# Splitting low-rank factors ahead of rescaling, summing x3 with its bias early, building rope tables on VectorE one round ahead, and turning the first queries among the embedding groups

## The reference

```python
x = x + L0_ffn(L0_cond(x, itok))          # weights picked by index, then an int4 matrix
x = x + L1_ffn(L1_cond(x, block_table, cache_seqlens))   # paged attention, then top-1 low-rank
x = x + L2_ffn(L2_cond(x, itok))          # indexed low-rank, then SiLU gate with low-rank terms
x = x + L3_ffn(L3_cond(x, language_ids))  # top-2 experts, then an int8 product

def L1_cond(x):                           # 32 query heads, 8 key/value heads, D = 128
    q, k, v = x @ Wq.T, x @ Wk.T, x @ Wv.T
    q, k = rope(rmsnorm(q, qw), pos), rope(rmsnorm(k, kw), pos)
    # rope: concat(t1 * cos - t2 * sin, t2 * cos + t1 * sin)
    keys, vals = concat(k_cache[block_table], k), concat(v_cache[block_table], v)
    return softmax(mask(q @ keys.T / sqrt(D))) @ vals @ Wo.T

def L3_ffn(t):                            # per-row int8 quantisation
    iscale = max(|t|) / 127
    q = clip(round(t / iscale), -127, 127)
    return (q @ qweight) * iscale * wscale + bias
```

## Time and profile before

| what | value |
|---|---|
| median of 3 runs | 3198.6 us (3192.68 to 3199.76) |
| the profiled execution: its time | 3195.55 us |
| its span, first to last instruction | 3193.8 us |
| PE busy | 3024.6 us, 95% of the span |
| DVE / ACT / POOL busy | 1552.8 / 1284.7 / 1490.8 us |
| mean granted TensorE clock | 0.981 |

### The profile page before, as it was taken

The page is one execution under the profiler, slowest core; times in us unless marked ns, Lnnn a source line. Parts: engine busy times, 40 slices in busy tenths (PEclk is TensorE's granted clock), DMA queues, the critical chain, the costliest instruction groups (busy, mean ns, idle before and its releaser), DMA issues. The chain is left out here.

```text
span 3193.8 us, 55792 instructions
## 1 busy us (share of the span) xinstructions
PE 3024.6 (95%) x15256; PEld 2022.0 (63%) x15264; DVE 1552.8 (49%) x3979; ACT 1284.7 (40%) x3014; POOL 1490.8 (47%) x1275
## 2 busy tenths in 40 slices
PE   3789999999999999999999999999999996999897
PEld 2466666666666666666666666666666674655554
DVE  5544444444444444444444444444444453656665
ACT  1344444444444444444444444444444441222222
POOL 7355555555555555555555555555555540000000
PEclk9899999999999999999999999999999998999998
DMA  8544444444444344545444444434444454211210
GB/s 291 203 115 122 121 121 121 121 119 120 118 118 118 118 118 118 198 119 169 122 119 119 119 119 119 119 119 119 119 119 119 119 150 164 49 40 31 49 30 13
DMA packets 416154, 377.54 MB, mean 118 GB/s; under 512 B 83427, under 2 KB 347763, under 8 KB 414996
## 3 DMA queue, kind: packets, MB, share of 16 engines
q1 hardware_dynamic: 358484, 186.81, 20.7%
q0 software_dynamic: 50480, 174.40, 17.5%
q10 hardware_dynamic: 7056, 14.46, 1.2%
HBM read 341.23 MB, written 25.85 MB: 115 GB/s over the span
## 5 line engine op out<-in xcount | busy, mean ns | idle before, releaser
L533 DVE CUSTOM_DVE_ANT_0 ps_s<-ps_s,mask 128x544 f32<-128x544 f32 x512 | 375.0, 733 | 940.6 <-PE ps_s L360 781.2
L262 POOL DMA_INDIRECT v_sb<-in_v_rows_w,v_row x504 | 489.7, 972 | 473.9 <-PE ps_oT L385 264.2
L319 PE MATMUL ps_t<-wqkv,xT 128*128 128x512 f32 x1488 | 701.6, 594 | 0.0
L383 PEld LDWEIGHTS ps_oT<-pT,v_sb 128*128 128x128 f32 x4096 | 528.4, 192 | 188.9 <-issue 188.2
L433 ACT ACTIVATE ps_s<-ps_s,nmax 128x544 f32<-128x544 f32 x512 | 352.3, 688 | 586.3 <-DVE nmax L533 519.9
L383 PE MATMUL ps_oT<-pT,v_sb 128*128 128x128 f32 x4096 | 543.1, 276 | 11.6 <-issue 11.5
L343 PE MATMUL ps_t<-wo,oT 128*128 128x512 f32 x1024 | 524.7, 596 | 2.5 <-ACT oT L448 0.9
L359 PE MATMUL ps_s<-k_sb,qT 128*128 128x416 f32 x1024 | 448.0, 519 | 11.4 <-issue 5.7
L448 ACT ACTIVATE oT<-ps_oT 128x128 f32<-128x128 f32 x512 | 142.7, 279 | 685.9 <-PE ps_oT L385 656.4
L543 DVE TENSOR_SCALAR p_sb<-ps_s,rinv 128x544 f32<-128x544 f32 x512 | 401.4, 784 | 23.8 <-DVE rinv L540 0.3
L368 PEld LDWEIGHTS ps_pT<-ident_sb,p_sb 128*128 128x128 f32 x2048 | 251.7, 141 | 187.4 <-issue 181.6
(11 more groups left out here) (219 smaller groups left out, 3545.5 us busy)
## 6 DMA issues: line engine op xcount, KB each, us to landing
k_sb<-in_kT SPq DMA_DIRECT2D x2048, 64.0 KB
v_sb<-in_v_rows_w,v_row POOLq DMA_INDIRECT x512
v_new<-v_raw SPq DMA_DIRECT2D x128, 64.0 KB, 1.9
wo<-in_wo_w POOLq DMA_DIRECT2D x2, 4096.0 KB, 15.2
y_scratch<-y_sb SPq DMA_DIRECT2D x32, 256.0 KB
xT<-x1T_scratch POOLq DMA_DIRECT2D x31, 256.0 KB
tab<-rope_scratch POOLq DMA_DIRECT2D x31, 256.0 KB
wqkv<-in_wqkv_w ACTq DMA_DIRECT2D x6, 1024.0 KB, 10.5
```

What stands on the lines that cost most here:

```text
L262: e.indirect_dma_start(out=v_sb[:, b % 2, c, :], out_offset=None, in_=A["v_rows_w"], in_offset=bass.IndirectOffsetOnAxis(ap=v_row[:, b, c: ...
L319: m = e.matmul(ps_t[bank_of(t)][:, :], xT[:, k, :], wqkv[:, k, 512 * t:512 * t + 512], start=k == 0, stop=k == KC - 1)
L383: e.matmul(ps_oT[:, :], v_sb[:, b % 2, c, h * D:(h + 1) * D], pT[:, u % 2, c, :], start=c == 0, stop=False)
L533: e.tensor_tensor_reduce(out=scores(u), in0=scores(u), in1=mask[:, b % 2, :], scale=-SCALE, scalar=3e38, op0=ALU.add, op1=ALU.min, accum_o ...
```

## The change

In the tail `split_low_rank(k + 1, p)` stands before `rescale(k, 1)`; x3 plus bias goes to a new tile `xb` while the next products run; `output(k, p)` is a single add and stands in pass k + 1, between `route` and `third`. SP issues the y loads ahead of the stores.

In the attention VectorE multiplies cosine and sine (`csn`, 64 KB a round, loaded where `tab` of 256 KB was) by the norm weights `w4`, in unit 1 of the round before the one that uses them (`make_tables`). In the embedding GpSimd no longer makes tables: ScalarE squares and scales the cosine, one store takes both, and VectorE makes the first table at g = 2. The angles wait for their own two loads and not for six, the first `spread` stands ahead of the unpacking, `x1` has three buffers, `turn` runs two groups behind, and the page loads and weight sums come earlier. The first round's five query and key tiles are turned by TensorE within the embedding, through two banks, and the waits for the stores of the stage move into the next stage. Clearing `v_new` moves from VectorE to GpSimd. Page numbers lie in four partitions.

```diff
+def make_tables(e, W, cosine, sine):
+    for i, t in enumerate((cosine, sine)):
+        part = lambda v: v[:, :, :].rearrange("p (s b) (h n) -> p s b h n", b=2, h=2)[:, :, i, :, :]
+        e.tensor_tensor(part(W.tab), t.unsqueeze(1).unsqueeze(1).broadcast_to([P, 2, 2, D // 2]), part(W.w4), ALU.mult).then_inc(W.tab_made, 1)
...
-            for t in range(NQT):
-                turn_q(0, t)
             score(0, 0, 0)
...
+            def table(r):
+                e.wait_ge(dma_tab, 16 * r)
+                e.wait_ge(rope_step, STEPS * r)
+                make_tables(e, W, csn[:, 0, :], csn[:, 1, :])
+
             def body(r):
                 for u in range(UNITS):
+                    if u == 1 and not last(r):
+                        table(r + 1)
                     if ahead(r, u, 2) is not None:
                         mask_scores(*ahead(r, u, 2))
...
-    PAGES_AT = {5: (0, 0), 6: (0, 1), 7: (0, 2), 8: (0, 3), 9: (1, 0), 10: (1, 1), 11: (1, 2), 12: (1, 3)}
-    SUMS_AT = {10: ("w2f", "w2"), 12: ("b2f", "b2")}
+    PAGES_AT = {3: (0, 0), 4: (0, 1), 5: (0, 2), 6: (0, 3), 7: (1, 0), 8: (1, 1), 9: (1, 2), 10: (1, 3)}
+    SUMS_AT = {7: ("w2f", "w2"), 8: ("b2f", "b2")}
...
-            e.wait_ge(out_fold, 32)
-            for i in range(2):
-                e.wait_ge(out_x[i], 16 * (GROUPS // 2))
-                e.wait_ge(out_xT[i], 16 * (GROUPS // 2))
...
-            tables(0)
             gather(2)
-            e.wait_ge(out_tab, 16)
-            tables(2)
+            e.wait_ge(trig, 4)
+            e.dma_start(tab_d.rearrange("g p k n -> p k g n"), cs_sn).then_inc(out_tab, 16)
...
+            def turn_q(t):
+                e.wait_ge(W.rope_step, STEPS1 if t < 3 else STEPS)
...
-                if g > 0:
-                    turn(g - 1)
+                if g > 1:
+                    turn(g - 2)
...
+                if g == GROUPS - 1:
+                    for t in range(3):
+                        turn_q(t)
+            turn(GROUPS - 2)
             turn(GROUPS - 1)
+            for t in range(3, NQT):
+                turn_q(t)
...
+            e.activation(cs, cs, ACT.Square).then_inc(trig, 1)
+            e.wait_ge(trig, 3)
+            e.activation(cs, cs, ACT.Copy, scale=-2.0, bias=1.0).then_inc(trig, 1)
...
-            e.wait_ge(dma_t, 16 * 6)
+            e.wait_ge(dma_a, 16 * 2)
...
+            e.wait_ge(bd_zero, 1)
+            spread(0)
             e.wait_ge(dma_q, 16 * 5)
...
-                wait(e, out_x[i], 16 * (g // 2))
-                wait(e, x1_turned, g - 1)
-                e.tensor_tensor(x1[:, i, :], xa[:, g % XB, :], s16[:, i, :], ALU.add).then_inc(x1_ready, 1)
+                wait(e, out_x[g % 3], 16 * (g // 3))
+                wait(e, x1_turned, g - 2)
+                e.tensor_tensor(x1[:, g % 3, :], xa[:, g % XB, :], s16[:, i, :], ALU.add).then_inc(x1_ready, 1)
...
+                for p in both:
+                    e.wait_ge(event["x3_ready"], 2 * k + p + 1)
+                    e.tensor_tensor(xb[p][:, :], x3[p][:, :], bias3[:, :], ALU.add).then_inc(event["x3_biased"], 1)
...
-                e.tensor_tensor(qf[p][:, :], qf[p][:, :], bias3[:, :], ALU.add).then_inc(event["d_biased"], 1)
-                e.wait_ge(event["d_biased"], 2 * k + p + 1)
+                e.wait_ge(event["x3_biased"], 2 * k + p + 1)
                 e.wait_ge(stored[p], 16 * (k + 1))
-                e.tensor_tensor(outb[p][:, :], qf[p][:, :], x3[p][:, :], ALU.add).then_inc(event["out_ready"], 1)
+                e.tensor_tensor(outb[p][:, :], qf[p][:, :], xb[p][:, :], ALU.add).then_inc(event["out_ready"], 1)
...
+                if not (isinstance(k, int) and k == 0):
+                    for p in both:
+                        output(k - 1, p)
                 third(k)
...
-                output(k, 0)
-                rescale(k, 1)
-                output(k, 1)
-                if more:
                     for p in both:
                         split_low_rank(k + 1, p)
+                rescale(k, 1)
```

## The result

The changed kernel takes 3136.16 us (median of 4 runs, 3134.53 to 3139.89) against 3198.47 for the kernel before beside it, ratio 0.9826 [0.9806, 0.9846]. It is faster by 62 us, where 73.4 (76 against the median) was forecast: the time lies in the range, 14 us above the predicted 3122. The profiled run took 3137.39 us, 58.2 less than the profiled run of before.

A forecast was written before the change was run, and what follows sets the result against it. Attention was taken as TensorE's own time, so gains had to come from TensorE's idle time in embedding and tail. Embedding 43.0, tail 30.4 and attention 0 sum to 73.4 us off 3195.55, giving 3122, range 3110 to 3140.

The forecast's parts named there:

- 3.9 less 0.4: Tail's end: pass 7 gains 3.9 us from the earlier gate work; the first last store, later by one add, costs 0.4.
- Both covers: Tail: existing VectorE waits hide the moved output adds (1.38 against 1.36 us) and the xb adds (1.38 in 2.39).
- rival 2: Tail: covers fail, adds costing 1.4 us a pass, or VectorE's gate work limits; gain 21, 3132 us; chance 0.10.
- Rival 3: Attention: GpSimd holds VectorE's table operations, 6.7 us in each of 31 rounds, 207 in all; 3329 us; chance 0.02.
- (b): Embedding, first product to first projection: held add and store wait give back 10.1 us, slow work 1.9; 12.0, from 8 to 14.
- (d): Embedding, last projection to first score: shorter wait 4.5 us, turning 7.5, earlier page issues 5; 17.0, from 11 to 20.
- (a): Embedding, up to the first product: it comes at 29.5 us, 14.0 earlier; 17.5 if ScalarE is no obstacle.
- The other term, 1.9: Embedding, within (b): estimated gain of 1.9 us because part of TensorE's work behind the hold ran slow.
- (c): Embedding: the six projections, 73.72 to 101.93 us, repeat unchanged; gain 0.
- The 5 for the groups: Embedding, within (d): earlier page issues free 5 us of 7.9 idle after the projections, bounds 0 and 7.9.
- The sign named in advance: Embedding: the prediction is wrong if TensorE waits for xa, stores or the fold weights between 30 and 100 us.
- rival 1: Embedding held elsewhere: DMA-bound stretch at 396 GB/s has no slack; gain about 27 us, 3138 us; chance 0.19.

The follow-up runs named there:

- experiments 2 and 3: Kernel before with only the tail's split moved, outputs left: 3171.21 us; kernel before with all tail edits plus eight unused semaphore increments ahead of the tail's loop: 3158.85 us.
- tail_only: Kernel before with all of the change's tail edits and none of the others: 3174.89 us, ratio 0.9953.
- Experiment 6: Changed kernel with ScalarE's Exp and its table load moved ahead of the last turned-query copies (group 15): 3137.42 us, ratio 0.9831.
- The last experiment: Changed kernel with five x buffers, later wqkv loads spread behind mix copies, and ScalarE's table load at group 11: 3119.39 us, ratio 0.9768.
- experiments 5 and 8: Changed kernel with wqkv loads spread behind mix copies: 3130.84 us; the same with five x buffers and ScalarE's table load at group 11: 3119.39 us.

## Why the prediction was right in part

**Tail, 30.4 forecast, 31.3 measured: right, term by term.** Passes 1 to 6 lost 26.1 (26.9 forecast by the length of pass 0), the end 4.6 (3.5 forecast, 3.9 less 0.4), and 0.7 lies ahead of pass 0, where nothing was forecast. Both covers held: passes with the output in front of their x3 add are 0.14 us longer than pass 0, which has none, so rival 2 is out. That both the split and the gate's start matter was argued then and is shown by experiments 2 and 3. It held for the layout that the changed kernel happened to have: in the layout of `tail_only` the same edits gave 17.3, and the prediction did not think of this.

**Attention, 0 forecast: right within the scatter.** Rival 3, the table held by GpSimd, is out: all 62 operations took 0.41 to 0.42 us. That the first profile had 4.5 us more misled me for one round of experiments, since one profile of this stage is worth no more than 6 us either way.

**Embedding, 43.0 forecast, 31.4 measured: the step that failed, (b) and (d).** (a) came as worked out, 30.05 against 29.5, with ScalarE's six issues, which end at 29.35, as the limit that the prediction named.

In (b), 43.50 to 73.72 became 30.05 to 54.37, 5.9 saved of 12.0. The sum gave TensorE the whole hold of VectorE and its wait for a store, 10.1. But TensorE's own row says that it stood 5.63 us for that add; ahead of this it had stood 3.79, until 53.70, for group 4's x, and VectorE's wait and hold began within that time. The 5.63 went and the wait for x grew from 3.79 to 4.83, since the buffer is free only when group 0 is summed: TensorE's idle time fell by 5.7, from 10.5 to 4.8. The other term, 1.9 for slow work behind the hold, gave 0.2 (19.73 to 19.49 us of work), as the work behind the remaining wait was slow again. With a fifth buffer the stretch is 17.1 us long and saves 13.1, which is what shows the wait for x as the cause.

(c) was 28.13 against 28.21. In (d), from the last projection's start to the first score, 43.34 became 31.35: 12.0 saved of 17.0. The 5 for the groups came, 5.1 by the rows of TensorE (28.7 to 23.5, the two turns counted that now stand between the queries'), though only about 1 of it from the waits for x, 5.25 to 4.28; the prediction took the idle time there for the page issues'. What failed is the end: of 12.0 forecast for the wait and the turns (14.66 us before) 6.9 came. A wait of 4.98 was to become a bare meeting of 0.5 and is 4.24. The meeting is 0.45 indeed, but 2.3 us of ScalarE's copies stand ahead of it, and 1.5 of its table load with the operation behind it, an edit of the diff that the sum passed over. Experiment 6 takes that 1.5 off the end. What the copies would give back was not tried.

The last experiment gets 41.1 of the forecast 43.0, but not by the forecast's terms: (b) saves 14.2 there and (d) 13.7. The sign named in advance, TensorE waiting for `xa` between 30 and 100 us, did appear. The mechanism left out was rival 1's, a wait elsewhere, and its 3138 us is nearer to the measured 3136 than the forecast's 3122. Its reason, that the stretch at 396 GB/s has no slack, does not hold: the wait went with as many GB/s, and experiments 5 and 8 ran the stretch from 20 to 50 us at 315 and 319.

In the whole, the stages explain the profiled run: 31.4 and 31.3 less 4.5 are its 58.2. That embedding and tail alone, 62.7, come so close to the medians' 62.3 is partly luck: on two other chips the gain was 58.1 and 63.4.

## What to carry to other kernels

Time for which one engine is held is not time for which the next one waits: before a hold is given back, read the idle time in the rows of the engine that ends the chain, and what else it waits for meanwhile. When a stall goes, ask for each load behind it when it is issued, not only how many bytes there are: a ring of buffers ties the load to the work of so many groups earlier, and work that comes sooner meets it. Work off the path (a table load, an output) is free only where its engine waits for another; look for that idle time in the timeline, not at a place that is early. Before a few microseconds of a long stage are explained, profile the same code twice, and put a stall at a loop's start next to the instruction queue's packets.

## What the runs showed of the hardware

A loop's place in an engine's program cost 14 us of 3170 in four passes: 4.6 to 4.9 us idle at each jump back and about 5 packets more a pass over the instruction queue. With eight more instructions ahead there was no such idle time, and 7 packets in all. No other layout that ran here had it in the tail; a comparison of two kernels can hold such a difference by accident, as that of the tail's edits alone did. The profile puts the idle time down to the last semaphore event, here ScalarE's, which had come 5 us before. A 256 KB load of x took 7.7 us beside others at 400 GB/s, and 6.6 right behind a single one of 1 MB. A wait of 4.83 us cost 7.2, as TensorE's work behind it ran at a lower granted clock (0.86 over the stretch in place of 1.00).
